# An LSTM with a low-rank adapter behind it: up product with tokens on partitions, and the residual added on TensorE

## The chip, the cores and the metric

The kernel runs on one core of one Trainium2 chip. The metric is the device time of an execution in microseconds (us). The median of three runs of the kernel before is 622.96 us (622.89 to 625.73).

## The reference

`x` has 16 batches of 256 tokens with 256 channels, all float32. First an LSTM runs over the 256 tokens, and its hidden states are added to `x`. Then an adapter, whose low-rank parts (rank 8) are made per batch from a condition vector, is applied, again with a residual.

```
def _L0_cond_ref(x, h0, Wx, Wh, b):
    xz = einsum('ntd,dk->ntk', x, Wx) + b
    step: z = xz_t + prev_h @ Wh;  ai, af, ao, ag = split(z, 4)
          i, f, o = sigmoid(ai), sigmoid(af), sigmoid(ao);  g = tanh(ag)
          next_c = f * prev_c + i * g;  next_h = o * tanh(next_c)

def _L1_cond_ref(x, ada_emb, base_up, base_down, ...):
    c = layernorm(ada_emb) * ln_gamma + ln_beta
    w = gelu(c @ W1 + bias1) @ W2 + bias2
    a1, b1, a2, b2 = [t.reshape(B, D, R) for t in split(w, 4)]
    u = einsum('btd,bdr->btr', x, a2)
    mid = gelu(einsum('btd,dl->btl', x, base_down) + einsum('btr,blr->btl', u, b2))
    v = einsum('blr,btl->btr', b1, mid)
    out = einsum('btl,kl->btk', mid, base_up) + einsum('bkr,btr->btk', a1, v)
    return x + out

x = x + _L0_cond_ref(x, cond_1024, Wx, Wh, b)
x = x + _L1_cond_ref(x, cond_1024, ...)
```

## The kernel before

The 256 tokens are cut into 32 blocks of `TB` = 8 tokens. A block of 8 tokens by 16 batches is 128 columns (or rows), which fills a 128-wide tile. `schedule` calls `one_block(k, front)` for every block on every engine; each engine has its own instruction stream, written out by hand, and the streams meet through semaphores. `front` is true for blocks 0 to 29. Inside a block there is a loop over the 8 recurrence steps `s`.

**The recurrence.** In each step PE computes the gates' inputs z from the hidden state h_t and `wh` (line 674: 32 narrow weight loads and products into the two `z` banks, then 16 into the `z_o` bank, each a 16-column tile). VectorE (DVE) transposes them (lines 821 and 825), ScalarE (ACT) takes the tanh of the gates (412, 418), VectorE makes products and the new cell (831, 836), ScalarE takes its tanh (424), and VectorE writes the two halves of h_t (843). PE waits for the first half before it starts the next z. Between z_o and the next z, PE's stream holds other work, called the filler here.

**The filler.** In front blocks one 256-wide piece of the input projection of block k + 2 closes every step's filler (`project`, line 496, bank `x_bank`). From block 4 on the adapter of the block before (`a = follower(k)`, lane 0) goes through the steps: `down_rank` in step 0 (u; line 507), `down_full` in steps 1 to 3 (six 128x128 products; line 522), `up_rank` in step 4 (v; line 529), `up_full` in steps 5 to 7 (six 128x128 products, channels on the partitions; line 545). All matmuls are float32. A float32 product appears in the trace as two LDWEIGHTS and two MATMUL instructions, a transpose as one of each. VectorE masks u and v (line 762), ScalarE does the GELU (346).

**The end of the adapter.** The up product leaves channels on partitions and tokens in the columns, in `out_bank`. `add_residual` (line 777, VectorE) adds `a.xp` (x + h of the block) and writes `y_t`. For blocks 4 to 28 that runs in step 2 of the block after, `transpose_y` (line 553, PE) turns its two halves in steps 3 and 4 back into `out_bank`, first in the filler, and `copy_y` (line 354, ScalarE) copies the result to `y_nat` in step 4, from where SP stores it. In the last blocks (`deferred` is false) the add is in step 6 of the same block, one transpose in step 7 and the other in step 0 of the block after.

**Early blocks.** The adapter's weights are not ready in the first blocks, so the adapter work of blocks 0 to 2 (`EARLY`) is kept for the end: `early(k)`, lane 1, with the bank `x_bank[1]` for the up product and `x_bank[0]` (free of projections then) for the rest, in blocks 30, 31 and in the tail behind the last block. There PE does `down_full(e)` as five products in step 1 and one in step 2. The tail is written out by hand: down, rank and up products of the last early block and of block 31, then adds, transposes and copies. `last_early` and `last` are these two jobs.

**POOL** adds h to x for each block (`add_h`, line 934) behind the last step of the block; before it overwrites `xp` it waits for the job that read it.

Of the kernel before, what the change touches and what calls it, by code (L numbers as in the profile page):

```python
# [54 lines left out]
def lstm_adapter(nc, x, cond, Wx, Wh, b, base_up, base_down, gamma, beta, W1, bias1, W2, bias2, out):  # L55
    ctx = ExitStack()
    with ctx:
# [64 lines left out]
        y_t = [sb(f"y_t{i}", [P, NM, P]) for i in lanes]  # L122
# [51 lines left out]
        out_psum, y_ready = ([sem(f"{n}{i}") for i in lanes] for n in ("out_psum", "y_ready"))  # L174
        yt_psum, y_copied = ([sem(f"{n}{i}") for i in lanes] for n in ("yt_psum", "y_copied"))
# [49 lines left out]

        def deferred(k):

            return k.plus(-1).k < NBLK - 2
# [91 lines left out]
        def _(act):  # L320
# [21 lines left out]
            def gelu_mid(a):  # L342
                act.wait_ge(mid_psum[a.lane], a.seq.k + 1)
                if a.seq.at_least(1):
                    act.wait_ge(out_psum[a.lane], a.seq.k)
# [4 lines left out]
            def copy_y(a):  # L350
                act.wait_ge(yt_psum[a.lane], a.seq.k + 1)
# [51 lines left out]
            def one_block(k, front):  # L403
                a, e, done = follower(k), early(k), follower(k.plus(-1))
                for s in range(TB):
# [47 lines left out]
                    if s == (4 if deferred(k) else 0) and done and done.seq.exists():  # L453
# [15 lines left out]
        def _(pe):  # L469
# [63 lines left out]
            def up_full(a, parts):  # L533

                for i in parts:
                    m, part = divmod(i, 3)
                    if i == 0:
# [4 lines left out]
                    cols = slice(m * P, (m + 1) * P)  # L542
                    lhs, rhs = ((up_t[:, part, cols], act_t[a.lane][:, part, :]) if part < 2 else
                                (a1_t[:, cols], v_own[a.lane][:, :]))
                    ins = pe.matmul(up_bank[a.lane][:, cols], lhs, rhs, start=(part == 0), stop=(part == 2))  # L545
                    if i == 5:
                        ins.then_inc(out_psum[a.lane], 1)

            def transpose_y(a, halves):
                if 0 in halves:  # L550
                    pe.wait_ge(y_ready[a.lane], a.seq.k + 1)
                for m in halves:
                    ins = pe.transpose(up_bank[a.lane][:, m * P:(m + 1) * P], y_t[a.lane][:, m, :], ident[:, :])  # L553
                if 1 in halves:
                    ins.then_inc(yt_psum[a.lane], 1)
# [87 lines left out]
            def one_block(k, front):  # L643
# [3 lines left out]
                for s in range(TB):  # L647
# [47 lines left out]
                    if a:  # L695
# [37 lines left out]
            transpose_y(follower(Blk(NBLK // 2 - 1, 1)), (1,))  # L733

# [237 lines left out]
```

## Time and profile before

| | |
|---|---|
| median of 3 runs | 622.96 us |
| the profiled execution | 622.3 us |
| its span, first to last instruction | 620.3 us |
| mean granted TensorE clock | 0.994 of full speed |
| PE busy | 600.6 us (97%) |
| PE weight loads (PEld) busy | 441.2 us (71%) |
| DVE busy | 478.7 us (77%) |
| ACT busy | 386.7 us (62%) |
| POOL busy | 38.2 us (6%) |

The times are of one execution on the chip. PE's products are pipelined and overlap, and their ends are modelled, so a busy PE is not one that has no room: how long an instruction occupies PE is read from the distance of starts. PEld is the weight load, which overlaps the products. An engine's idle time is given in brackets in the timeline, with what ended it. Where a helper records the operation its line is the helper's.

### The profile page before, as it was taken

What the parts mean: (1) busy time and instruction counts of PE and PEld (TensorE: products, weight loads), DVE (VectorE), ACT (ScalarE), POOL (GpSimd) and SP (SyncE); (2) the same over time, 40 slices, a digit from 0 to 9 for tenths busy, and PEclk for the clock granted to TensorE, in tenths of its full rate; (3) what the DMA queues carried; (4) which work ended last, traced back from release to release, by engine and by line L of the source; (5) the groups of instructions that cost most, each with busy time, mean ns of one, the idle gap of its engine ahead of it and who ended that gap; (6) DMA issues with size and microseconds to landing.
All of it is one profiled execution on the core that took longest, in us unless ns stands there. A gap on an engine that the chain in (4) does not pass through costs nothing.

```text
span 620.3 us, 34579 instructions
## 1 busy us (share of the span) xinstructions
PE 600.6 (97%) x14176; PEld 441.2 (71%) x14176; DVE 478.7 (77%) x2548; ACT 386.7 (62%) x2158; POOL 38.2 (6%) x78
## 2 busy tenths in 40 slices
PE   8789999999999999999999999999999999999997
PEld 5565555777777777777777777777777777777886
DVE  3566666888888888888888888888888888888773
ACT  2365555666666666666666666666666666666662
POOL 3000000000000000000000000000000000000000
PEclk9799999999999999999999999999999999999999
DMA  5893530232222113232321232322023232321201
GB/s 159 231 218 142 180 45 12 38 46 54 55 54 39 35 39 54 55 54 54 54 36 25 53 54 54 54 54 45 26 43 54 55 54 54 54 37 21 47 20 35
DMA packets 31471, 38.74 MB, mean 62 GB/s; under 512 B 3601, under 2 KB 29505, under 8 KB 30290
## 3 DMA queue, kind: packets, MB, share of 16 engines
q1 hardware_dynamic: 31282, 36.51, 27.4%
q8 instruction: 112, 1.84, 1.3%
q14 instruction: 45, 0.37, 0.2%
q0 software_dynamic: 32, 0.03, 0.0%
HBM read 15.55 MB, written 4.19 MB: 32 GB/s over the span
## 4 chain that ended last, share of the span: by engine, by line
PE 85%; DVE 7%; POOL 4%; issue 2%; DMA 1%; SPq 0%; POOLq 0%; ACT 0%; DVEq 0%; ACTq 0%
PE z L674 32%; PE x_bank L496 17%; PE aux L522 8%; PE z_o L674 7%; PE out_bank L545 5%; PE out_bank L603 4%; POOL xp L934 4%; PE aux L507 3%; PE aux L474 2%; PE out_bank L553 2%; PE aux L529 2%; DVE z L821 2%; DVE prod L831 1%; DVE gates L836 1%; DVE h_t L843 1%
## 5 line engine op out<-in xcount | busy, mean ns | idle before, releaser
L674 PEld LDWEIGHTS z<-wh,h_t 128*16 128x16 f32 x8160 | 155.1, 96 | 119.6 <-DVE h_t L843 96.0
L674 PE MATMUL z<-wh,h_t 128*16 128x96 f32 x8160 | 228.1, 248 | 5.6 <-DVE h_t L843 2.3
L821 DVE STREAM_TRANSPOSE z<-z 128x96 f32<-128x96 f32 x512 | 151.5, 298 | 87.2 <-PE z L674 60.3
L412 ACT ACTIVATE gates<-z 128x48 f32<-128x48 f32 x512 | 107.7, 210 | 141.9 <-DVE z L821 114.3
L496 PE MATMUL x_bank<-wx,x_t 128*128 128x256 f32 x512 | 156.2, 393 | 0.5 <-ACT x_t L330 0.5
L336 ACT ACTIVATE z<-seed 128x96 f32<-128x96 f32 x512 | 123.7, 242 | 5.6 <-DMA seed<-proj 5.6
L674 PE MATMUL z_o<-wh,h_t 128*16 128x64 f32 x4080 | 105.7, 219 | 0.4
L831 DVE SCALAR_TENSOR_TENSOR prod<-gates 128x32 f32<-128x32 f32 x512 | 97.8, 191 | 0.6
L836 DVE SCALAR_TENSOR_TENSOR gates<-prod 128x16 f32<-128x16 f32 x512 | 84.3, 165 | 8.7
L496 PEld LDWEIGHTS x_bank<-wx,x_t 128*128 128x128 f32 x512 | 80.7, 195 | 6.4 <-issue 1.5
L674 PEld LDWEIGHTS z_o<-wh,h_t 128*16 128x16 f32 x4080 | 80.6, 97 | 1.2 <-issue 0.9
L340 ACT ACTIVATE z_o<-seed 128x64 f32<-128x64 f32 x256 | 58.3, 228 | 33.8 <-DVE h_t L843 2.3
L418 ACT ACTIVATE gate_o<-z_o 128x32 f32<-128x32 f32 x256 | 50.4, 197 | 29.2 <-DVE z_o L825 7.5
L825 DVE STREAM_TRANSPOSE z_o<-z_o 128x64 f32<-128x64 f32 x256 | 65.8, 257 | 0.5 <-PE z_o L674 0.4
L934 POOL TENSOR_TENSOR xp<-x_t,h_t 128x128 f32<-128x128 f32 x58 | 29.4, 528 | 494.0 <-DVE h_t L843 494.0
L756 DVE TENSOR_TENSOR proj<-x_bank,b_all 128x256 f32<-128x256 f32 x128 | 53.8, 420 | 5.3 <-PE x_bank L496 5.1
L843 DVE SCALAR_TENSOR_TENSOR h_t<-gate_o,tanc 128x16 f32<-128x16 f32 x256 | 43.8, 171 | 13.3 <-ACT tanc L424 1.2
L843 DVE SCALAR_TENSOR_TENSOR h_t<-gate_o,z_o 128x16 f32<-128x16 f32 x256 | 43.8, 171 | 9.2
L424 ACT ACTIVATE tanc<-gates 128x16 f32<-128x16 f32 x256 | 46.7, 182 | 0.0
L424 ACT ACTIVATE z_o<-gates 128x16 f32<-128x16 f32 x256 | 46.1, 180 | 0.1
L522 PE MATMUL aux<-xp,down 128*128 128x128 f32 x232 | 43.1, 288 | 0.0
L545 PE MATMUL out_bank<-act_t,up_t 128*128 128x128 f32 x232 | 42.8, 289 | 0.0
(109 smaller groups left out, 445.9 us busy)
## 6 DMA issues: line engine op xcount, KB each, us to landing
seed<-proj SPq DMA_DIRECT2D x128, 128.0 KB, 4.0
w<-in_L_cond_W SPq DMA_DIRECT2D x4, 2048.0 KB, 9.9
x_nat<-in_x SPq DMA_DIRECT2D x32, 128.0 KB, 4.0
out<-y_nat SPq DMA_DIRECT2D x32, 128.0 KB, 3.7
wx<-in_L_cond_Wx SPq DMA_DIRECT2D x2, 512.0 KB, 5.6
wh<-in_L_cond_Wh SPq DMA_DIRECT2D x2, 256.0 KB, 6.5
wh<-in_L_cond_Wh SPq DMA_DIRECT2D x1, 512.0 KB, 6.2
w<-in_L_cond_W SPq DMA_DIRECT2D x1, 256.0 KB, 4.3
```

What stands on the lines that cost most here:

```text
L336: act.activation(z_bank[m][:, 0:GC], seed[buf][:, s, GC * m:GC * (m + 1)], ACT.Copy)\
L412: act.activation(gates[s % 2][m][:, 0:3 * B].rearrange("p (g b) -> p g b", b=B), zt[m].rearrange("p (g c) -> p g c", c=C)[:, :, 0:B], ACT. ...
L424: act.activation(tanc[m], gates[(s + 1) % 2][m][:, 3 * B:4 * B], ACT.Tanh, scale=0.5).then_inc(tanc_ready[m], 1)
L496: ins = pe.matmul(x_bank[q % 2][:, 0:XW], x_t[f.k % N_X][:, kc, :], wx[:, kc, q * XW:(q + 1) * XW], start=(kc == 0), stop=(kc == 1))
L522: ins = pe.matmul(mid_bank[a.lane][:, cols], lhs, rhs, start=(part == 0), stop=(part == 2))
L545: ins = pe.matmul(up_bank[a.lane][:, cols], lhs, rhs, start=(part == 0), stop=(part == 2))
L674: ins = pe.matmul(dst, h_prev[:, kc, :], rhs, start=False, stop=(kc == 1), skip_group_check=True)
L821: dve.transpose(zt[m], z_bank[m][:, 0:GC]).then_inc(turned[m], 1)
L825: dve.transpose(zt_o, o_bank[:, 0:OC]).then_inc(turned_o, 1)
L831: dve.scalar_tensor_tensor(prod[m][:, :], now[:, 0:2 * B], 1.0, now[:, 2 * B:4 * B], ALU.add, ALU.mult).then_inc(prod_ready[m], 1)
L836: dve.scalar_tensor_tensor(gates[(s + 1) % 2][m][:, 3 * B:4 * B], prod[m][:, B:2 * B], 0.5, prod[m][:, 0:B], ALU.mult, ALU.add).then_inc(c ...
L843: dve.scalar_tensor_tensor(h_t[k.par][:, m, s, 0:B], gate_o[:, B * m:B * (m + 1)], 1.0, tanc[m], ALU.add, ALU.mult).then_inc(ht_ready[m], 1)
```

## The change

The up product is turned around: the activations (and the masked v) are now the stationary operand and `up_t` (and `a1_t`) the moving one, 256 columns wide, so that tokens come out on the partitions. Three wide products take the place of six narrow ones. The residual is added in the same PSUM region, by two products with `a.xp` as the stationary operand and the identity as the moving one (`x0`, `x1`, 128 columns each). `add_residual`, `y_t` and `transpose_y` are gone. In front blocks l0, l1 and v are in steps 5, 6 and 7, x0 and x1 in steps 3 and 4 of the block after; block 30 follows the same plan, in block 31 x0 and x1 come in step 7. The GELU that overwrites `act_t` waits for l1 alone (`act_used`). The early blocks' down product is three and three, the first rank product of `last_early` moves from step 7 to step 6 of block 31 with its mask, and the tail is in another order.

```diff
-            def up_full(a, parts):
-                for i in parts:
-                    m, part = divmod(i, 3)
...
-            def transpose_y(a, halves):
...
+            def up_full(a, parts, whole=False):
+                y = up_bank[a.lane]
+                for part in parts:
+                    if part == "l0":
+                        if a.seq.at_least(1):
+                            pe.wait_ge(y_copied[a.lane], a.seq.k)
+                        pe.wait_ge(up_ready, 2)
+                        pe.wait_ge(act_ready[a.lane], a.seq.k + 1)
+                    if part == "v":
                         pe.wait_ge(v_ready[a.lane], a.seq.k + 1)
...
+                    lhs, rhs, lo = {"l0": (act_t[a.lane][:, 0, :], up_t[:, 0, :], 0),
+                                    "l1": (act_t[a.lane][:, 1, :], up_t[:, 1, :], 0),
+                                    "v": (v_own[a.lane][:, :], a1_t[:, :], 0),
+                                    "x0": (a.xp[:, 0, :], ident[:, :], 0),
+                                    "x1": (a.xp[:, 1, :], ident[:, :], P)}[part]
+                    width = P if part in ("x0", "x1") else D
+                    ins = pe.matmul(y[:, lo:lo + width], lhs, rhs, start=(part == "l0"),
+                                    stop=(whole and part == parts[-1]), skip_group_check=True)
+                    if part == "l1":
+                        ins.then_inc(act_used[a.lane], 1)
+                if whole:
+                    ins.then_inc(y_psum[a.lane], 1)
...
-                    if done and done.seq.exists():
-                        if not deferred(k) and s == 0:
-                            transpose_y(done, (1,))
-                        if deferred(k) and s in (3, 4):
-                            transpose_y(done, (s - 3,))
-                    if s == 7 and not front and k.p == 1:
+                    if done and done.seq.exists() and s in (3, 4):
+                        up_full(done, ("x0",) if s == 3 else ("x1",), whole=(s == 4))
+                    if s == 6 and not front and k.p == 1:
                         pe.wait_ge(v_ready[1], last_early.seq.k)
                         down_rank(last_early)
...
-                        if front and s in (5, 6, 7):
-                            up_full(a, range(2 * s - 10, 2 * s - 8))
-                        if not front and s in (5, 6):
-                            up_full(a, range(3 * s - 15, 3 * s - 12))
-                        if not front and s == 7:
-                            transpose_y(a, (0,))
+                        if s >= 5:
+                            up_full(a, (("l0",), ("l1",), ("v",))[s - 5])
+                        if s == 7 and not front and k.p == 1:
+                            up_full(a, ("x0", "x1"), whole=True)
...
                         if s in (1, 2):
-                            down_full(e, range(0, 5) if s == 1 else range(5, 6))
+                            down_full(e, range(3 * s - 3, 3 * s))
...
                         if s in (4, 5, 6):
-                            up_full(e, range(2 * s - 8, 2 * s - 6))
+                            up_full(e, (("l0",), ("l1",), ("v",))[s - 4])
                         if s == 7:
-                            transpose_y(e, both)
+                            up_full(e, ("x0", "x1"), whole=True)
...
             schedule(one_block)
-            transpose_y(follower(Blk(NBLK // 2 - 1, 1)), (1,))
-            down_full(last_early, range(0, 4))
+            down_full(last_early, range(6))
             down_rank(last)
-            down_full(last_early, range(4, 6))
-            down_full(last, range(0, 3))
             up_rank(last_early)
-            down_full(last, range(3, 6))
-            up_full(last_early, range(0, 3))
+            down_full(last, range(6))
+            up_full(last_early, ("l0", "x0", "x1"))
             up_rank(last)
-            up_full(last_early, range(3, 6))
-            up_full(last, range(6))
-            transpose_y(last_early, both)
-            transpose_y(last, both)
+            up_full(last_early, ("l1", "v"), whole=True)
+            up_full(last, ("l0", "x0", "x1", "l1", "v"), whole=True)
...
-            def add_residual(a):
-                dve.wait_ge(out_psum[a.lane], a.seq.k + 1)
-                dve.tensor_tensor(y_t[a.lane][:, :, :], a.xp[:, :, :],
...
                 if k.at_least(EARLY + 2):
-                    pool.wait_ge(y_ready[0], k.k - EARLY - 1)
+                    pool.wait_ge(y_psum[0], k.k - EARLY - 1)
```

## Rows read from the trace of the kernel before

**Rows 1.** The page's chain by engine; who waited for whom (us, times, longest).

```profile
PE 85%; DVE 7%; POOL 4%; issue 2%; DMA 1%; SPq 0%; POOLq 0%; ACT 0%; DVEq 0%; ACTq 0%
...
PEld z L674 <- DVE h_t L843: 96.0, 242, 0.9
```

**Rows 2.** Timeline, block 15, steps 3 to 6: start, us, engine, line, operation.

```profile
309.63 0.67 PEld L674 LDWEIGHTS z<-wh,h_t 128*16 128x16 f32 x32 [0.42 <-DVE h_t L843]
...
309.71 0.41 DVE L777 TENSOR_TENSOR y_t<-xp,out_bank 128x256 f32<-128x256 f32 x1
...
310.69 0.33 PE L553 MATMUL out_bank<-ident,y_t 128*128 128x128 f32 x1
...
310.86 0.39 PE L522 MATMUL aux<-xp,down 128*128 128x128 f32 x2
...
311.30 0.60 PE L496 MATMUL x_bank<-wx,x_t 128*128 128x256 f32 x2
...
311.62 0.17 DVE L843 SCALAR_TENSOR_TENSOR h_t<-gate_o,tanc 128x16 f32<-128x16 f32 x1
...
311.85 0.67 PEld L674 LDWEIGHTS z<-wh,h_t 128*16 128x16 f32 x32 [0.35 <-DVE h_t L843]
...
316.27 0.67 PEld L674 LDWEIGHTS z<-wh,h_t 128*16 128x16 f32 x32 [0.35 <-DVE h_t L843]
```

**Rows 3.** Timeline of PE: last projection product before z, steps 3 and 0.

```profile
311.52 0.38 PE L496 MATMUL x_bank<-wx,x_t 128*128 128x256 f32 x1
...
304.95 0.38 PE L496 MATMUL x_bank<-wx,x_t 128*128 128x256 f32 x1
305.25 0.28 PE L674 MATMUL z<-wh,h_t 128*16 128x96 f32 x4
```

**Rows 4.** Timeline, block 15, step 2: first two products of the filler.

```profile
308.47 0.49 PE L522 MATMUL aux<-u_own,b_t 128*128 128x128 f32 x2
...
308.80 0.39 PE L522 MATMUL aux<-xp,down 128*128 128x128 f32 x2
```

**Rows 5.** Lines 553 and 545: durations in ns, min/median/max.

```profile
L553 PE MATMUL x_bank<-ident,y_t x6: 272/273/273, 588.9 to 616.2; 128*128 128x128 f32 x6
...
L545 PE MATMUL out_bank<-v_own,a_t x116: 275/275/377, 121.2 to 615.9; 128*128 128x128 f32 x116
```

**Rows 6.** Timeline of PE's weight loads, block 31, steps 5 to 7.

```profile
601.68 0.67 PEld L674 LDWEIGHTS z<-wh,h_t 128*16 128x16 f32 x32 [0.19 <-DVE h_t L843]
...
604.05 0.62 PEld L674 LDWEIGHTS z<-wh,h_t 128*16 128x16 f32 x32
...
605.05 0.52 PEld L545 LDWEIGHTS out_bank<-act_t,up_t 128*128 128x128 f32 x4
...
606.36 0.13 PEld L674 LDWEIGHTS z<-wh,h_t 128*16 128x16 f32 x8
```

**Rows 7.** Timeline, starts of z in block 30: steps 1 to 3, and block 31.

```profile
573.49 0.66 PEld L674 LDWEIGHTS z<-wh,h_t 128*16 128x16 f32 x32
...
576.28 0.63 PEld L674 LDWEIGHTS z<-wh,h_t 128*16 128x16 f32 x32
...
578.45 0.67 PEld L674 LDWEIGHTS z<-wh,h_t 128*16 128x16 f32 x32 [0.42 <-DVE h_t L843]
...
589.99 0.67 PEld L674 LDWEIGHTS z<-wh,h_t 128*16 128x16 f32 x32 [0.91 <-DVE h_t L843]
```

**Rows 8.** Timeline, block 30, step 5: first half of h_t.

```profile
585.22 0.17 DVE L843 SCALAR_TENSOR_TENSOR h_t<-gate_o,tanc 128x16 f32<-128x16 f32 x1 [0.40 <-ACT tanc L424]
```

**Rows 9.** Timeline of the tail.

```profile
607.37 0.52 PEld L507 LDWEIGHTS x_bank<-xp_early,a_w 128*128 128x128 f32 x4
...
610.96 0.38 ACT L346 ACTIVATE act_t<-x_bank 128x256 f32<-128x256 f32 x1 [1.85 <-PE x_bank L522]
...
617.20 0.38 ACT L354 ACTIVATE y_nat<-out_bank 128x256 f32<-128x256 f32 x1 [0.35 <-PE out_bank L553]
```

**Rows 10.** The page's group of the projection's bias add: busy, mean ns.

```profile
L756 DVE TENSOR_TENSOR proj<-x_bank,b_all 128x256 f32<-128x256 f32 x128 | 53.8, 420 | 5.3 <-PE x_bank L496 5.1
```

More of the change, by code:

```diff
@@ L121, in lstm_adapter @@
         act_t = [sb(f"act_t{i}", [P, 2, P]) for i in lanes]
-        y_t = [sb(f"y_t{i}", [P, NM, P]) for i in lanes]
         y_nat = [[sb(f"y_nat{lane}_{i}", [P, D]) for i in range(2)] for lane in lanes]
@@ L173, in lstm_adapter @@
         v_psum, v_ready = ([sem(f"{n}{i}") for i in lanes] for n in ("v_psum", "v_ready"))
-        out_psum, y_ready = ([sem(f"{n}{i}") for i in lanes] for n in ("out_psum", "y_ready"))
-        yt_psum, y_copied = ([sem(f"{n}{i}") for i in lanes] for n in ("yt_psum", "y_copied"))
+        act_used = [sem(f"act_used{i}") for i in lanes]
+        y_psum, y_copied = ([sem(f"{n}{i}") for i in lanes] for n in ("y_psum", "y_copied"))
         stored = [[sem(f"stored{lane}_{i}") for i in range(2)] for lane in lanes]
@@ L224, in early @@
             return Job(Blk(0, 0, n), 1) if 0 <= n < EARLY else None
-        def deferred(k):
-            return k.plus(-1).k < NBLK - 2
         end = Blk(NBLK // 2, 0)
@@ L344, in gelu_mid @@
                 if a.seq.at_least(1):
-                    act.wait_ge(out_psum[a.lane], a.seq.k)
+                    act.wait_ge(act_used[a.lane], a.seq.k)
                 act.activation(act_t[a.lane][:, :, :],
@@ L350, in copy_y @@
             def copy_y(a):
-                act.wait_ge(yt_psum[a.lane], a.seq.k + 1)
+                act.wait_ge(y_psum[a.lane], a.seq.k + 1)
                 if a.seq.at_least(2):
@@ L452, in one_block @@
                         gelu_mid(a)
-                    if s == (4 if deferred(k) else 0) and done and done.seq.exists():
+                    if s == 4 and done and done.seq.exists():
                         copy_y(done)
@@ L531, in up_rank @@
                 ins.then_inc(v_psum[a.lane], 1)
-            def up_full(a, parts):
-                for i in parts:
-                    m, part = divmod(i, 3)
-                    if i == 0:
+            def up_full(a, parts, whole=False):
+                y = up_bank[a.lane]
+                for part in parts:
+                    if part == "l0":
                         if a.seq.at_least(1):
@@ L540, in up_full @@
                         pe.wait_ge(up_ready, 2)
+                        pe.wait_ge(act_ready[a.lane], a.seq.k + 1)
+                    if part == "v":
                         pe.wait_ge(v_ready[a.lane], a.seq.k + 1)
[L542 to L547, printed above, removed]
-            def transpose_y(a, halves):
[L550 to L555, printed above, removed]
+                    lhs, rhs, lo = {"l0": (act_t[a.lane][:, 0, :], up_t[:, 0, :], 0),
[10 more added lines that the diff above has]
+                    ins.then_inc(y_psum[a.lane], 1)
             def make_weights(k, s):
@@ L772, in mask_v @@
                 mask(mid_bank[a.lane], v_own[a.lane], v_ready[a.lane])
-            def add_residual(a):
-                dve.wait_ge(out_psum[a.lane], a.seq.k + 1)
-                dve.tensor_tensor(y_t[a.lane][:, :, :], a.xp[:, :, :],
-                                  up_bank[a.lane][:, 0:NM * P].rearrange("p (m t) -> p m t", m=NM), ALU.add)\
-                   .then_inc(y_ready[a.lane], 1)
             dve.memset(zeros[:, :], 0.0).then_inc(zeroed, 1)
@@ L864, in one_block @@
             def one_block(k, front):
-                a, e, f, done = follower(k), early(k), k.plus(2), follower(k.plus(-1))
+                a, e, f = follower(k), early(k), k.plus(2)
                 for s in range(TB):
@@ L877, in one_block @@
                     new_hidden(k, s, 0, n)
-                    if s == 7 and not front and k.p == 1:
+                    new_hidden(k, s, 1, n)
+                    if s == 6 and not front and k.p == 1:
                         mask_u(last_early)
-                    new_hidden(k, s, 1, n)
                     if s == 0 and a:
@@ L889, in one_block @@
                         mask_v(a)
-                    if s == 2 and deferred(k) and done and done.seq.exists():
-                        add_residual(done)
-                    if s == 6 and a and not front:
-                        add_residual(a)
-                    if s == 6 and e:
-                        add_residual(e)
                     if not k.at_least(1) and s < 2:
@@ L908, in _ @@
             mask_v(last)
-            add_residual(last_early)
-            add_residual(last)
         @block.gpsimd
```

## The prediction

> **What bounds the kernel now.** I read the chain of waits first, then who waits for whom. The chain is 85% PE, but in the second view PE waits for the hidden state 242 times [rows 1]: in most of the 256 recurrence steps PE's other work, the "filler" issued behind the gate products, is done before h_t. So I went to the timeline of one ordinary block. There a step lasts 2.21 to 2.22 us (z loads at 309.63 and 311.85; three steps on, at 316.27, 6.64 after the first). The half of h_t that PE waits for ends at 311.62 + 0.17 = 311.79 and z follows 0.06 later: the loop h_t, z, transpose, gates, cell, h_t sets the step. Filler starts 1.06 after z (310.69) [rows 2].
>
> How much room has the filler? The last x_bank product of that step starts at 311.52, 0.33 before z. In the step where POOL holds the filler up and PE is late, the same product starts 0.30 before z (304.95, 305.25) [rows 3]. So in the steps whose filler is a transpose, two narrow products and the projection, PE has only 0.03 us to spare. What an edit adds to PE in such a step lengthens it; what it takes off VectorE counts only where h_t or a transpose has waited for it.
>
> **The change, part by part.**
>
> 1. *Residual add on VectorE goes* (32 of 0.41 us). It begins at 309.71 behind h_t and ends at 310.12, and the next gate transpose can't begin before z's products are through; the step with it is as long as the others [rows 2]. Hidden by that wait, so worth 0. Bounds: 0 and a gain of 0.41 each, if it had held a transpose up, which the equal step lengths exclude in the ordinary blocks. The two of the tail are in part 5.
>
> 2. *Up product with tokens on partitions, steps 5 to 7.* Six 128-wide products (12 PE instructions) become three 256-wide ones (6). A narrow instruction costs 0.11 in a stream: the four of two narrow products take 0.44 (310.86 to 311.30). A wide one has the x_bank product as its row: its halves start at 311.30 and 311.52, 0.22 apart [rows 2, 3]. 12 x 0.11 = 1.32 against 6 x 0.22 = 1.32: PE time is the same, and the steps wait for h_t anyway. Worth 0; bounds -0.1 to +0.1 per block in PE time, and 0 in the step time while the 0.03 holds.
>
> 3. *Two transposes become two identity products, steps 3 and 4 of the next block.* They stand first in the filler. A transpose is one instruction, and the product behind it starts 0.17 later (310.69, 310.86) [rows 2]. An ordinary narrow product is two instructions, and when it stands first, the product behind it starts 0.33 later (308.47, 308.80) [rows 4]. So each swap costs 0.16 of PE where 0.03 is free. The move of the residual from VectorE, which had room, to PE, which has none, is the core of the case.
>
> Step by step, with ten narrow instructions of filler as the nearest rows (1.10 by 0.11 each; the new filler, six narrow and two wide, is 0.66 + 0.44, the same). Such filler runs 1.31 from its start to z (605.05, 606.36), of which 0.21 is getting started and the way out; I take 1.30 for the new one. Step 3: 1.06 + 1.30 = 2.36. Step 4 starts with z late, so that both halves of h_t are there and its filler starts 1.00 after z (604.05, 605.05) [rows 6]: 1.00 + 1.30 = 2.30. Step 5 gets 0.04 back, 2.17, as after the other late step (576.28, 578.45) [rows 7]. Sum 6.83 against 6.64: +0.19 per block. The pair of measured steps agrees: 2.37 and 2.31 with ten instructions [rows 6]. Blocks 5 to 29 do this, 25 of them: **+4.8 us**. Bounds: 0, if the swap costs no more than the 0.03, and 25 x 2 x 0.16 = +8.0, if no lateness comes back. I take 4.8, since the row of a late step shows what comes back.
>
> Two rules of the Trainium skill bear on this swap, and they pull apart. "TensorE: Matmul & The Clock Gate", Part 4, prices a 128x128 transpose at some 275 ns in a kernel, most of it latency; the trace's duration of a transpose, 0.273, agrees, and it is that of an ordinary narrow product, 0.275 [rows 5], so by this rule the swap costs nothing and the 25 blocks add 0. "FP8 and Floating Point Precision", TensorE Precision Notes, says true FP32 takes four passes through the array; an estimate from it is three more passes of 128 columns at 2.4 GHz, 0.16 per swap, which gives the 4.8. Starts, not durations, say how long PE is taken, and they side with the second.
>
> 4. *Blocks 30 and 31, where early blocks 0 and 1 are worked in beside the last ones.* Early down product: ten instructions in step 1 and two in step 2 become six and six. Block 30 from z at 573.49 to 589.99 is 16.50 now, with 2.79 in step 1 [rows 7]. New: step 1 has ten instructions, 1.04 + 1.31 = 2.35; step 2 ten and late, 2.32; step 3 ten (identity, down, rank), 2.32; step 4 six narrow and two wide, 2.31; step 5 four wide, 2.17, plus the 0.36 by which VectorE paused there in this execution [rows 8], 2.53; steps 6 and 7 2.21 and 2.23 as an ordinary and as the present one. Sum 16.27: **-0.23**. The pause is left in both, being no part of the change. Block 31 up to z at 606.36 is 16.37 now. New: 2.34 for step 0 as now, 2.32 three times, 2.31, 2.17, and 2.56 for step 6, which gains the first rank product of the last early block: four narrow and four wide, 0.63 + 0.41 + 1.51. Sum 16.34: **-0.03**. Bounds for both: -0.8 (every added ten-instruction step hidden) and +0.5 (a further late step in each).
>
> 5. *Tail.* From the start of the last step's filler to the last copy 617.20 - 607.37 = 9.83 pass [rows 9]. Afterwards PE runs 14 wide and 52 narrow instructions there, 14 x 0.22 + 52 x 0.11 = 8.80 (wide: v of block 30's job and both last up products; narrow: eight identity instructions there and eight later, the two down products with 24, three groups of four for rank products). It must stop for the first GELU, whose rank product now stands right behind four instructions: that GELU takes 0.38 (610.96) [rows 9], and with 0.4 of handing over on both sides (my estimate from the 0.06 that PE needs after h_t and the 0.28 that a product takes to come out) 0.78 pass, against 0.56 of PE's other work: 0.22. Starting up, semaphores and the last product's way out I put at 0.5. Sum 9.52. Gone are the residual add and the transposes at the very end, but the full early down product now stands ahead of the last block's rank product and eats most of that. **-0.3**, bounds -1.0 (no stop, add and transposes all gained) and +0.6 (a second stop as long as the first plus a semaphore).
>
> 6. *Waits.* The identity products need no wait (a.xp and the bank are ready), the l0 product waits for act_t alone, and the v mask is asked for two steps later: all come later than what they wait for. POOL's h add waits for y_psum of step 4 instead of y_ready of step 2; it is asked for after step 7, over 6 us later. On ACT the copy stands at the same place. Worth 0, bounds 0 and 0.1 per block.
>
> Sum: 4.8 - 0.23 - 0.03 - 0.3 = +4.2 us. The profiled span 620.3 becomes 624.5, its execution 622.3 becomes 626.5. The median shown is 0.66 above that execution, so I predict **627.2** (+0.7%).
>
> **The rivals.**
>
> *A, the swap is free.* PE loads the weights of the identity product, which waits for nothing, while the z_o products still run, or a transpose occupies PE as long as its duration says. Then step 3 stays at 2.21 and only parts 4 and 5 count: 622.96 - 0.56 = **622.4**, not slower. For it: equal durations [rows 5]. Against: the down product that stands first in rows 4 waits for nothing either and still has its 0.33. It decides once the swap costs under 0.07 (0.03 room, and 0.04 that come back).
>
> *B, the late step also blocks VectorE.* In step 3 VectorE adds the bias to the projection, 0.42 long [rows 10], once the last x_bank product is through. With PE late that is z - 0.30 + 0.38 = z + 0.08, so the add ends near z + 0.52, and the gate transpose wants VectorE at z + 0.59. If the signal comes more than 0.07 later than I count, the transpose waits too: say 0.1 per block, 25 x 0.1 = 2.5, **629.7**. Against: the 0.07 are there by the rows.
>
> *C, half is paid.* The lateness of step 3 is not carried into step 4, because pauses of other engines or the copies' places widen the room: 0.10 per block, **624.9**.
>
> **How the numbers follow.** Forecast 0.64, A 0.16, B 0.08, C 0.12. About 0.5% (3.1 us) is what a measurement of this kernel can tell from no change. Slower by more: nearly all of the forecast (its own range is 625.0 to 629.2) and B, 0.69. Within: A, C and a rest of the forecast, 0.27. Faster by more: 0.04, if the pauses of 0.36, of which there are a handful, fall away on top of A. The range 622.3 to 629.4 takes A in and leaves out B and the tails.
>
> **What would show it.** Right: in the middle blocks steps 3 and 4 last 2.35 and 2.30, with z 0.19 behind the end of h_t instead of 0.06, step 5 lasts 2.17 and the rest 2.21, and a block is 17.96 instead of 17.77. The identity product takes 0.33 before its neighbour. Wrong: steps 3 and 4 stay at 2.21 (A), or the idle time of VectorE before the gate transpose of step 4 is gone and the transpose starts over 0.63 after z (B). In blocks 30 and 31 step 1 must fall from 2.8 to 2.35.

## The result, and the profile after

The changed kernel takes 628.5 us (median of 4 executions, 627.69 to 629.49) against 623.2 us for the kernel before on the same chip: ratio 1.0072, 95% interval 1.0041 to 1.0104. It is slower by some 0.7%, with an interval clear of 1, and lies within the forecast's range (627.2 us, 622.3 to 629.4). The profiled execution took 627.69 us with a span of 625.9, at a mean granted clock of 0.995 (before: 0.994), so the clock has no part in the difference of the two profiles.

The page after, sections 1 and 4 (busy time of the engines; the chain by engine):

```profile
span 625.9 us, 34291 instructions
...
PE 606.4 (97%) x14048; PEld 445.3 (71%) x14048; DVE 469.9 (75%) x2516; ACT 387.1 (62%) x2158; POOL 38.3 (6%) x78
...
PE 86%; DVE 6%; POOL 4%; issue 2%; DMA 1%; SPq 0%; POOLq 0%; ACT 0%; DVEq 0%; ACTq 0%
```

And who waited for whom (us, times, longest):

```profile
PEld z L669 <- DVE h_t L820: 97.3, 246, 0.9
```

VectorE has 8.8 us less to do than before (469.9 against 478.7) and the kernel is 5 us slower. These rows don't say why. The waits for the hidden state still look as in [rows 1], 246 times instead of 242, though in 50 of these steps PE itself is now late. The list counts every weight load that had to wait at all, and in the late steps, too, it shows 0.33 us of idle time put down to h_t (below, 333.00). The lengths of the steps have to be read. The timeline of an ordinary block (16; start, us, engine, line, operation; z of steps 3, 4, 5 and 6 and what stands in step 3; answers to [rows 2]):

```profile
330.65 0.67 PEld L669 LDWEIGHTS z<-wh,h_t 128*16 128x16 f32 x32 [0.42 <-DVE h_t L820]
...
331.70 0.49 PE L545 MATMUL out_bank<-ident,xp 128*128 128x128 f32 x2
...
332.03 0.39 PE L517 MATMUL aux<-xp,down 128*128 128x128 f32 x2
...
332.47 0.60 PE L491 MATMUL x_bank<-wx,x_t 128*128 128x256 f32 x2
...
332.64 0.17 DVE L820 SCALAR_TENSOR_TENSOR h_t<-gate_o,tanc 128x16 f32<-128x16 f32 x1
...
333.00 0.63 PEld L669 LDWEIGHTS z<-wh,h_t 128*16 128x16 f32 x32 [0.33 <-DVE h_t L820]
...
333.11 0.42 DVE L740 TENSOR_TENSOR proj<-x_bank,b_all 128x256 f32<-128x256 f32 x1
...
333.59 0.63 DVE L798 STREAM_TRANSPOSE z<-z 128x96 f32<-128x96 f32 x2
...
335.31 0.63 PEld L669 LDWEIGHTS z<-wh,h_t 128*16 128x16 f32 x32 [0.33 <-DVE h_t L820]
...
337.48 0.67 PEld L669 LDWEIGHTS z<-wh,h_t 128*16 128x16 f32 x32 [0.37 <-DVE h_t L820]
```

Step 3 lasts 2.35 (330.65 to 333.00), step 4 2.31, step 5 2.17. The first half of h_t ends at 332.64 + 0.17 = 332.81 and z follows 0.19 later, where in [rows 2] it followed after 0.06: PE is what ends last. The identity product begins at 331.70 and the next product at 332.03, 0.33 later, where the transpose of [rows 2] let its neighbour start after 0.17. From the start of the filler to z pass 1.30 us.

The durations don't give this price. The group of the identity products (line 545, durations in ns, min/median/max), and that of the transposes before, in the same bank (line 553):

```profile
L545 PE MATMUL out_bank<-ident,xp x116: 273/275/377, 133.2 to 621.6; 128*128 128x128 f32 x116
...
L553 PE MATMUL out_bank<-ident,y_t x58: 273/329/333, 132.3 to 616.9; 128*128 128x128 f32 x58
```

58 identity products give 116 instructions with a median of 275 ns; the 58 transposes gave 58 with a median of 329. The 273 of [rows 5] is that of six transposes in the other bank. At the head of a filler a transpose takes 329 ns, and a product's first instruction 377; behind other products the two take 273 and 275. None of these is the time for which PE is taken: that is read from the starts.

Starts of z in blocks 30 and 31 (steps 1 to 6 of block 30, step 0 and step 7 of block 31), to be held against [rows 7] and [rows 6]:

```profile
580.13 0.62 PEld L669 LDWEIGHTS z<-wh,h_t 128*16 128x16 f32 x32
...
582.45 0.63 PEld L669 LDWEIGHTS z<-wh,h_t 128*16 128x16 f32 x32
...
584.77 0.62 PEld L669 LDWEIGHTS z<-wh,h_t 128*16 128x16 f32 x32
...
587.09 0.63 PEld L669 LDWEIGHTS z<-wh,h_t 128*16 128x16 f32 x32
...
589.39 0.63 PEld L669 LDWEIGHTS z<-wh,h_t 128*16 128x16 f32 x32 [0.33 <-DVE h_t L820]
...
591.56 0.67 PEld L669 LDWEIGHTS z<-wh,h_t 128*16 128x16 f32 x32 [0.43 <-DVE h_t L820]
...
596.05 0.67 PEld L669 LDWEIGHTS z<-wh,h_t 128*16 128x16 f32 x32 [0.27 <-DVE h_t L820]
...
612.37 0.62 PEld L669 LDWEIGHTS z<-wh,h_t 128*16 128x16 f32 x32 [0.33 <-DVE h_t L820]
```

The tail: its first filler product, the GELU of the last early block, the product that waits for it, the last copy (answers to [rows 9]):

```profile
613.38 0.30 PEld L545 LDWEIGHTS out_bank<-a_t,v_own 128*128 128x128 f32 x2
...
616.34 0.39 ACT L341 ACTIVATE act_t<-x_bank 128x256 f32<-128x256 f32 x1 [0.68 <-PE x_bank L517]
...
616.78 0.52 PEld L524 LDWEIGHTS x_bank<-act_t,b_w 128*128 128x128 f32 x4 [0.22 <-ACT act_t L341]
...
622.80 0.38 ACT L349 ACTIVATE y_nat<-out_bank 128x256 f32<-128x256 f32 x1 [1.36 <-PE out_bank L545]
```

The balance of the two profiled spans, from the starts of z (us). "Scattered" is what blocks 5 to 29 took beyond 25 times the sum of their median steps:

| stretch | before | after | difference | forecast |
|---|---|---|---|---|
| start to z of block 5 | 124.38 | 125.47 | +1.09 | 0 |
| blocks 5 to 29, 25 x (17.767; 17.961) | 444.17 | 449.03 | +4.85 | +4.8 |
| the same blocks, scattered | 2.69 | 3.29 | +0.60 | 0 |
| block 30 | 18.75 | 18.26 | -0.49 | -0.23 |
| block 31 to z of its step 7 | 16.38 | 16.32 | -0.06 | -0.03 |
| from there to the last copy | 10.83 | 10.43 | -0.40 | -0.3 |
| last copy to the end | 3.08 | 3.07 | -0.01 | 0 |
| span | 620.3 | 625.9 | +5.6 | +4.2 |

### The profile page after: what moved, and what is told of

The parts are those of the page before. It is cut to its first block, busy times and chain, and to the rows that moved or that the text cites. A ratio compares the mean times of both kernels' runs of the same rounds, so it can differ in the third digit from the quotient of the medians.

```text
span 625.9 us, 34291 instructions
## 1 busy us (share of the span) xinstructions
PE 606.4 (97%) x14048; PEld 445.3 (71%) x14048; DVE 469.9 (75%) x2516; ACT 387.1 (62%) x2158; POOL 38.3 (6%) x78
## 4 chain that ended last, share of the span: by engine, by line
PE 86%; DVE 6%; POOL 4%; issue 2%; DMA 1%; SPq 0%; POOLq 0%; ACT 0%; DVEq 0%; ACTq 0%
PE z L669 31%; PE x_bank L491 17%; PE out_bank L545 9%; PE aux L517 8%; PE z_o L669 7%; POOL xp L903 4%; PE out_bank L598 4%; PE aux L502 3%; PE aux L469 2%; PE aux L524 2%; DVE z L798 2%; DVE prod L808 1%; DVE gates L813 1%; DVE h_t L820 1%; DVE z_o L802 1%
## 5 line engine op out<-in xcount | busy, mean ns | idle before, releaser
L669 PEld LDWEIGHTS z<-wh,h_t 128*16 128x16 f32 x8160 | 156.9, 96 | 116.5 <-DVE h_t L820 97.3
L491 PEld LDWEIGHTS x_bank<-wx,x_t 128*128 128x128 f32 x512 | 87.2, 196 | 10.7 <-issue 1.5
L545 PE MATMUL out_bank<-up_t,act_t 128*128 128x256 f32 x116 | 35.1, 385 | 0.0
```

Source lines behind the costliest of these rows:

```text
L491: ins = pe.matmul(x_bank[q % 2][:, 0:XW], x_t[f.k % N_X][:, kc, :], wx[:, kc, q * XW:(q + 1) * XW], start=(kc == 0), stop=(kc == 1))
L545: ins = pe.matmul(y[:, lo:lo + width], lhs, rhs, start=(part == "l0"), stop=(whole and part == parts[-1]), skip_group_check=True)
L669: ins = pe.matmul(dst, h_prev[:, kc, :], rhs, start=False, stop=(kc == 1), skip_group_check=True)
```

## The experiments

My theory: the whole loss is the kind of PE work that the residual is made of. Where a step's filler has 0.03 us to spare, two instructions in place of one make it late, and the place in the block hardly matters. The turned up product and the add taken off VectorE are worth nothing. The rivals: the late steps come from the wide products or their neighbourhood; the add's going is a gain that something eats; the identity product's price is one of its place behind z_o. All step lengths below are medians over blocks 5 to 29, from the starts of z, as in the balance; the kernel before has 2.32 2.17 2.21 2.21 2.21 2.21 2.21 2.21 for steps 0 to 7. Each ratio is to the kernel before on the same chip; its medians in the three sets were 623.55 (e1 to e4), 623.71 (a0_again, e5 to e7) and 623.14 (e8, e1_again). A ratio isn't the quotient of the two medians (in a0_again that is 1.0059, the ratio 1.0048), but every interval holds both.

### e1_transpose_acc: the changed kernel with the residual as accumulating transposes

```diff
                     ins = pe.matmul(y[:, lo:lo + width], lhs, rhs, start=(part == "l0"),
+                                    is_transpose=(part in ("x0", "x1")),
```

> The changed kernel, with x0 and x1 as float32 transposes that accumulate onto the up product (one PE instruction each instead of two); nothing else differs, VectorE still adds nothing. My theory (the swap costs 0.16 us of PE where 0.03 is free): the filler of steps 3 and 4 runs 1.14 instead of 1.30, these steps fall from 2.35 and 2.31 to 2.21, a middle block from 17.96 to 17.77 (-4.9 us over 25 blocks), and with the fewer instructions in blocks 30, 31 and the tail the kernel comes to 622.4 us, ratio to before about 0.999. Rival (the loss comes from the wide products, the missing wait or the other order of the work, not from the identity products): it stays near 628.

Measured: 622.43 us, ratio 0.9978 [0.9958, 0.9998] (two of the twelve executions took 1063 and 2976 us; the ratio leaves them out, and without them the median is 622.09). Steps 3 and 4 are 2.213 and 2.212, the median block is 17.771. PE in step 3 of block 16:

```profile
329.67 0.33 PE L545 MATMUL out_bank<-ident,xp 128*128 128x128 f32 x1
...
329.84 0.39 PE L517 MATMUL aux<-xp,down 128*128 128x128 f32 x2
...
330.83 0.28 PE L670 MATMUL z<-wh,h_t 128*16 128x96 f32 x4
```

The count is x1, the neighbour starts 0.17 later, z 1.16 after the filler's start instead of 1.30. One word in one call takes the whole loss away; everything else of the change is still there.

### e2_before_product: the kernel before with its transposes as ordinary products

```diff
-                    ins = pe.transpose(up_bank[a.lane][:, m * P:(m + 1) * P], y_t[a.lane][:, m, :], ident[:, :])
+                    ins = pe.matmul(up_bank[a.lane][:, m * P:(m + 1) * P], y_t[a.lane][:, m, :], ident[:, :],
+                                    start=True, stop=True)
```

> The kernel before, with the two transposes of y done as ordinary products with the identity (two PE instructions each instead of one); the add on VectorE, the narrow up product and the old end stay. My theory: this alone makes steps 3 and 4 last 2.35 and 2.31, a middle block 17.96, +4.9 us, and some +0.4 in blocks 30 and 31: 628.5 us, ratio 1.0085. Rival (a transpose takes PE as long as a product, as their equal durations say): 623.2, no change.

Measured: 627.84 us, ratio 1.0064 [1.0044, 1.0083]; steps 3 and 4 2.349 and 2.306, block 17.961. Starts of z, steps 3 to 6 of block 16:

```profile
328.01 0.67 PEld L675 LDWEIGHTS z<-wh,h_t 128*16 128x16 f32 x32 [0.42 <-DVE h_t L844]
...
330.36 0.62 PEld L675 LDWEIGHTS z<-wh,h_t 128*16 128x16 f32 x32 [0.33 <-DVE h_t L844]
...
332.67 0.62 PEld L675 LDWEIGHTS z<-wh,h_t 128*16 128x16 f32 x32 [0.33 <-DVE h_t L844]
...
334.83 0.67 PEld L675 LDWEIGHTS z<-wh,h_t 128*16 128x16 f32 x32 [0.35 <-DVE h_t L844]
```

So the loss of the middle blocks can be put into the kernel before by this edit alone, to the hundredth of a step: 2.35, 2.31, 2.16. Together with e1 this is the cause from both sides.

### e3_before_balanced: the kernel before with the early down product three and three

```diff
-                            down_full(e, range(0, 5) if s == 1 else range(5, 6))
+                            down_full(e, range(3 * s - 3, 3 * s))
```

> The kernel before, with the early blocks' down product as three and three products in steps 1 and 2 instead of five and one. My theory: in blocks 30 and 31 step 1 falls from 2.80 and 2.77 to 2.36 and 2.32, step 2 rises from 2.17 to 2.32 and step 3 from 2.21 to 2.17 after a late step: -0.3 each, 622.6 us in all, too small for the clock but plain in the trace. Rival (the products of step 1 were hidden): no change of z's starts.

Measured: 622.21 us, ratio 0.9978 [0.9955, 1.0]. Starts of z in block 30, steps 1 to 4:

```profile
573.79 0.67 PEld L674 LDWEIGHTS z<-wh,h_t 128*16 128x16 f32 x32
...
576.15 0.62 PEld L674 LDWEIGHTS z<-wh,h_t 128*16 128x16 f32 x32
...
578.47 0.63 PEld L674 LDWEIGHTS z<-wh,h_t 128*16 128x16 f32 x32
...
580.64 0.67 PEld L674 LDWEIGHTS z<-wh,h_t 128*16 128x16 f32 x32
```

Steps 1 to 3 are 2.36, 2.32 and 2.17 where they were 2.80, 2.17 and 2.21: 0.33 less per block in blocks 30 and 31, 0.7 us in all. The trace shows the gain; the times can't show 0.7 us surely, as the interval ends at 1.0.

### e4_double: the identity products twice

```diff
-                        up_full(done, ("x0",) if s == 3 else ("x1",), whole=(s == 4))
+                        up_full(done, ("x0", "x0") if s == 3 else ("x1", "x1"), whole=(s == 4))
```

> The changed kernel, with x0 and x1 of the front blocks done twice in their steps (the residual counts twice there, so the result differs). My theory: steps 3 and 4 are PE-bound already, so each added narrow product costs its full 0.22: step 3 2.57, step 4 2.53, +0.45 per block and +11.2 us over the 25 blocks, +0.45 each in blocks 30 and 31 or a little less: about 640.5 us. Rival C of the prediction (room of some other kind swallows part of what is added): clearly less, 634 or so.

Measured: 638.41 us, ratio 1.0234 [1.0204, 1.0265]. Steps 3 and 4 are 2.570 and 2.530, block 18.405. Step 3 of block 16:

```profile
335.73 0.90 PE L669 MATMUL z<-wh,h_t 128*16 128x96 f32 x32
...
336.78 0.71 PE L545 MATMUL out_bank<-ident,xp 128*128 128x128 f32 x4
...
337.33 0.39 PE L517 MATMUL aux<-xp,down 128*128 128x128 f32 x2
...
338.30 0.34 PE L669 MATMUL z<-wh,h_t 128*16 128x96 f32 x5
```

The second product costs 0.22 a step, full price (0.55 to the neighbour's start instead of 0.33): once the room is gone each further narrow float32 product is paid whole, and the next step gives back no more than the 0.04. The 25 blocks account for 0.444 x 25 = 11.1 us over the changed kernel. Blocks 30 and 31 add 0.9 more (18.70 and 16.79 against 18.26 and 16.32), and the scattered time is 1.4 less (1.9 against 3.3). The total is 11.0 above the 627.4 that the next run gives for the changed kernel; the expected 640.5 had been built on its first median of 628.5 and was 2.1 too high.

### a0_again: the changed kernel a second time

> The changed kernel once more, beside the other three. Step theory: steps 3 and 4 of a middle block again 2.35 and 2.31, the kernel 627 to 629 us. Open is the stretch up to block 5, which took 1.1 us longer in the first profile than before: if that belongs to the change, it is there again; if it is the loading of the inputs, which varies from run to run, it lies anywhere between 123.4 and 125.5.

Measured: 627.37 us (10 executions), ratio 1.0048 [1.0024, 1.0072]. The steps are the same within 0.004 us (2.350, 2.306), but block 5 starts at 123.41, where it started at 125.47 in the first profile and at 124.38 in the kernel before. So the start-up of one kernel varies by 2 us, and the +1.09 of the balance's first line needs no effect of the change. It isn't excluded either: block 5 starts between 123.41 and 126.34 in the eight profiles without the add on VectorE, and between 123.42 and 124.50 in the four with it. The two sets put the loss at +0.5 and +0.7%, 3.7 and 5.3 us.

### e5_narrow: the wide up products cut in two

```diff
+                    halves = ((lo, lo + P),) if width == P else ((0, P), (P, D))
+                    for c, (at, to) in enumerate(halves):
+                        ins = pe.matmul(y[:, at:to], lhs, rhs if width == P else rhs[:, at:to],
```

> The changed kernel with each 256-wide product of the up product cut into two of 128 columns: twelve PE instructions in steps 5 to 7 again, tokens still on partitions. My theory (a wide instruction takes PE twice as long as a narrow one): the filler of steps 5 and 6 is 1.14 instead of 1.13, both under the 1.16 there are, steps stay 2.17 and 2.21, time 628.5, the same within 0.3 us. Rival (the wide products save or cost PE time): steps 5 to 7 change by over 0.02.

Measured: 626.93 us beside 627.37 for the uncut kernel on the same chip (1.006 [1.0039, 1.0081] and 1.0048 [1.0024, 1.0072]); the median block is 17.960 against 17.956. Twelve narrow instructions or six wide ones: no difference in these blocks, where steps 5 to 7 wait for h_t anyway. The cut does cost PE a little: in step 5 the last projection product starts 0.33 before z instead of 0.35, so the filler is nearly 0.02 longer, and in the tail, where PE ends last, the stretch from z of step 7 to the last copy is 10.53 in its profile against 10.43 in both of the uncut kernel.

### e6_added_step1: the same extra work in a step that had none

To e1 a transpose of 65536 times the identity and a product with its negative are added at the head of step 1's filler; together they add zero to the up bank, but for rounding on the diagonal. (The edit also makes the two tiles, once, at the start.)

```diff
+                    if front and done and done.seq.exists() and s == 1:
+                        pe.wait_ge(big_made, 2)
+                        pe.matmul(up_bank[0][:, 0:P], big[:, :], ident[:, :], start=False, stop=False,
+                                  is_transpose=True, skip_group_check=True)
+                        pe.matmul(up_bank[0][:, 0:P], minus_big[:, :], ident[:, :], start=False, stop=False,
+                                  skip_group_check=True)
```

> The kernel with x0 and x1 as accumulating transposes, and two more products added in step 1 of the front blocks, onto the same half of the bank: a transpose of 65536 times the identity and an ordinary product with minus it, which cancel. My theory: the filler of step 1 grows from 1.08 by 0.11 + 0.22 to 1.41; step 1, which starts late, goes from 2.17 to 2.42, step 2 gets 0.04 back, +0.20 per block, 25 blocks +5.1: 627.5 us. Rival (step 1 has room enough, as it has neither a transpose nor the residual): no change, 622.4.

Measured: 624.59 us, ratio 1.0016 [0.9984, 1.0049]. PE in step 1 of block 16:

```profile
326.84 0.33 PE L682 MATMUL out_bank<-ident,big 128*128 128x128 f32 x1
...
327.01 0.39 PE L684 MATMUL out_bank<-ident,minus_big 128*128 128x128 f32 x2
...
327.23 0.61 PE L522 MATMUL aux<-xp,down 128*128 128x128 f32 x4
...
328.20 0.34 PE L675 MATMUL z<-wh,h_t 128*16 128x96 f32 x5
```

Step 1 became 2.370, not 2.42, and step 2 2.169, so a block grows by 0.14 (3.6 us over the 25) instead of 0.20. The mechanism held, its size didn't. Filler to z is 1.36 here. The same filler without the pair (two narrow products and the projection) would take 1.07 if it set z: in step 1 of the kernel before, its last projection product starts 0.77 after its first product, and z follows 0.31 after that one where PE is late (here 2.370 - 2.063). So the pair costs 0.29. The product is 0.22 of it (327.01 to 327.23), which leaves 0.06 to 0.07 for the transpose, where I had set 0.11. A transpose at the head of the filler costs less than its distance to the neighbour, since that distance holds a delay that any first product has (0.33 - 0.22 = 0.11 for an ordinary one). The loss is read from the steps; the time's own interval holds 1, and the scattered time is 2 us less than in e1's profile (3.0 against 5.0).

### e7_steps_1_2: the identity products in other steps

```diff
-                    if done and done.seq.exists() and s in (3, 4):
-                        up_full(done, ("x0",) if s == 3 else ("x1",), whole=(s == 4))
+                    if done and done.seq.exists() and s in (1, 2):
+                        up_full(done, ("x0",) if s == 1 else ("x1",), whole=(s == 2))
```

> The changed kernel with x0 and x1 in steps 1 and 2 of the block after instead of 3 and 4, where the filler without them is as long (1.08) and has the same 0.09 of room. My theory, that only the sum of the filler in a step counts: step 1 2.31, step 2 2.31, step 3 2.17, step 4 2.21, +0.19 per block as in steps 3 and 4: 628.3 us. Rival (the place matters: products that stand behind a late step are caught up): under 626.

Measured: 626.83 us, ratio 1.0043 [1.0017, 1.0069]. Starts of z in block 16, steps 1 to 4:

```profile
327.42 0.63 PEld L669 LDWEIGHTS z<-wh,h_t 128*16 128x16 f32 x32 [0.33 <-DVE h_t L820]
...
329.74 0.62 PEld L669 LDWEIGHTS z<-wh,h_t 128*16 128x16 f32 x32 [0.33 <-DVE h_t L820]
...
332.04 0.62 PEld L669 LDWEIGHTS z<-wh,h_t 128*16 128x16 f32 x32 [0.33 <-DVE h_t L820]
...
334.21 0.67 PEld L669 LDWEIGHTS z<-wh,h_t 128*16 128x16 f32 x32 [0.42 <-DVE h_t L820]
```

2.32, 2.30 and 2.17 here, as medians 2.306, 2.306 and 2.170, block 17.953: the lateness moves with the product, and a different place saves nothing. In blocks 30 and 31, whose steps 1 and 2 also hold the early down product, it costs: these steps become 2.54 instead of 2.32, 0.5 us for both blocks. Steps 1 to 3 all hold two narrow products and the projection, 1.07 of the 1.16 us between the filler's start and z. The 0.09 left take a transpose at the head (0.06 to 0.07, and 0.02 to 0.03 are over, the room of the forecast) and not a product (0.22, late by 0.13).

### e8_add_kept: the add back on VectorE, in a kernel with free transposes

To e1 the 128x256 add (of `xp` and the up bank) is put back in step 2, into a scratch tile, and PE waits for it before x0.

```diff
+                    if done and done.seq.exists() and s == 3:
+                        pe.wait_ge(peeked, done.seq.k + 1)
...
+                    if s == 2 and done and done.seq.exists():
+                        dve.wait_ge(v_in_y, done.seq.k + 1)
+                        dve.tensor_tensor(scratch[:, :, :], done.xp[:, :, :],
```

> The kernel with accumulating transposes, with the 128x256 add of the kernel before kept on VectorE in step 2 of the block after (into a scratch tile that nobody uses), and PE waiting for it before x0, as it did before. My theory (the add lies in time in which VectorE waits for z): step 2 and 3 stay 2.21, a middle block 17.77, the time is that of the kernel without it, 622.4 to 623. Rival (taking the add off VectorE gave something back, and the loss was larger than it looks): +0.1 to +0.4 per block, 625 or more. Beside it: the pauses of 0.36 between the gate transposes and h_t sat at block 12 step 0 and block 28 step 0 in all seven profiles of kernels without the add and at block 24 step 7 and block 30 step 5 in the two others and the one before; if they hang on the place in VectorE's instruction stream, they move back towards these here.

Measured: 620.57 us, ratio 0.9973 [0.9953, 0.9994], median block 17.764. The add is there, behind step 2's work on VectorE in block 16: z of step 3 starts at 326.14 and z of step 4 at 328.35, 2.21 later:

```profile
326.20 0.41 DVE L872 TENSOR_TENSOR scratch<-xp,out_bank 128x256 f32<-128x256 f32 x1
```

27 of the adds are back and no step is longer for them: with them the kernel is, if anything, quicker.

### e1_again: e1 on the chip of e8

> The kernel with accumulating transposes once more, for its ratio to before. By the steps it should differ from before only in blocks 30 and 31 and the tail, about -1.5 us by the first profiles: ratio 0.9975, and pauses again at block 12 step 0 and block 28 step 0. If the first ratio of 0.9978 was chance, it comes out at 1.

Measured: 623.11 us, ratio 0.9992 [0.9972, 1.0012]. My expectation of 0.9975 lies in the interval, but the interval now holds 1 as well, so e1 is not shown to be faster than the kernel before. What the traces show is this: from z of block 30 to the last copy e1 takes 43.9 us against 46.0 before, so the end gains 2.0 us, and the scattered time of blocks 5 to 29 is 5.0 and 4.6 in its two profiles against 2.7. In e8 it is 3.1. About 1 us of the difference to before is in the pauses of VectorE that are told of at the end. Most of the rest is in PE's own stream, which stands between two gate products in a few steps, as here in step 3 of block 12 in e1_transpose_acc; e1_again has the same 0.45 of idle time before the same two products:

```profile
257.21 0.40 PE L670 MATMUL z_o<-wh,h_t 128*16 128x64 f32 x14
258.06 0.28 PE L670 MATMUL z_o<-wh,h_t 128*16 128x64 f32 x2 [0.45 <-issue]
```

That step is 0.69 longer than the others of its kind, in both. What PE does there isn't shown.

## Why the prediction was right

The forecast's mechanism held, step by step, and its sizes nearly so; the case was decided in part 3. That the second set's median, 627.37, lies 0.2 from the forecast is in part luck: the end came out 0.4 better than forecast, and the kernel before measured 0.8 more there than the 622.96 that the forecast started from.

**Part 1, the add.** Worth 0, as said: e8 puts it back in the middle blocks and nothing gets longer there (17.764 against 17.771 per block). Profile and run agree that the wait for z's products hides it.

**Part 2, the wide product.** Worth 0 in a block: e5 undoes the width with 17.960 against 17.956, and e2, which has the whole old up product beside the new kind of residual work, takes 17.961 as the changed kernel does.

**Part 3, the swap.** Forecast 2.36, 2.30 and 2.17 for steps 3 to 5 and +0.19 per block; measured medians 2.346, 2.306 and 2.172, +0.194. The terms of the swap come out as 0.22 for the product and 0.06 for the transpose, 0.16 as forecast, though the forecast took this difference from 0.33 and 0.17. e2 has the loss without the rest of the change, e1 has the rest without it. The room is nearer 0.02 than 0.03: the last projection product starts 0.328 before z in the step with the transpose and 0.307 in the late ones (medians). Of the two rules weighed there, the price by passes of "FP8 and Floating Point Precision" (the Trainium skill, TensorE Precision Notes) is the one that the runs bear out: its estimate was 0.16 per swap. The 275 ns of "TensorE: Matmul & The Clock Gate" (the Trainium skill, Part 4) agrees with the 273 of transposes behind other products. The forecast read its agreement from six of these alone; the 58 in `out_bank` have a median of 329. Neither is a price of PE time.

**Part 4, blocks 30 and 31.** The forecast steps of block 30 were 2.35, 2.32, 2.32, 2.31, then 2.17 without the pause; the rows above give 2.32, 2.32, 2.32, 2.30, 2.17 from step 1. Block 31 from 596.05 to 612.37 is 16.32, forecast 16.34. Steps 1 to 7 of block 30 took 15.92 (580.13 to 596.05) against 16.50 before. I forecast 16.27, with the pause of 0.36 in step 5 [rows 8] left in; without it that is 15.91, and in the profile after it isn't there. Step 0, which I had left alone, grew by 0.09 (2.25 to 2.34), so that the whole block gave -0.49.

**Part 5, the tail.** 622.80 - 613.38 = 9.42 where I had 9.52 (before 9.83). PE stops for the GELU as forecast: its next product comes at 616.78, 616.34 + 0.39 = 616.73 after it, and the bracket shows 0.22 of idle time, my figure for the stop. What made the rest 0.1 shorter isn't separated.

**Part 6, the waits.** The one wait of POOL that is put down to the up bank is that of the last add, at 614.66, and the second half of h_t, which it needs as well, ends at 614.69; PE's only stop behind it is the one for the GELU. Worth 0. The others of POOL's adds for `xp` wait for h_t, as before.

**The rivals.** A (the swap is free) falls by the rows of block 16 and by e2. Its step lengths are those of e1. That e1 also measured the 622.4 that I gave it, 622.43, is chance: its repeat gave 623.11, and it has fewer instructions in blocks 30, 31 and the tail than A supposes. Whether it would decide under 0.07, as I put it, isn't tested: no run has a price between 0 and 0.16. B (VectorE blocked as well) falls: with the bias add at 333.11 to 333.53 the gate transpose starts at 333.59, 0.59 after z, no later than the 0.63 of steps without lateness. Only 0.06 lie between the two, so it was near. C (half paid) falls with medians of 2.35 and 2.31.

What is left of the first profile, 5.6 against 4.2, is 1.1 before block 5, which a0_again shows to vary by more, 0.6 of scattered pauses, and the better end.

## What to carry to other kernels

Before moving work to an engine, measure how much room it has in the step that receives it, against a step in which it is known to be late: here 0.02 to 0.03 us a step decided 4 to 5 us, while 0.4 us on the other engine was worth nothing. Read what an instruction costs from the distance of starts, with its place in the stream (first or in the middle), since durations don't show it: 273 and 275 ns stood here for a transpose that cost 0.06 us and for one of the two instructions of a product that cost 0.22. Where a transposed operand has to be added to a float32 sum, try the transpose itself as the accumulating instruction before an identity product, and look at the result's values.

## What the runs showed of the hardware

**A float32 transpose as the accumulating instruction.** In e1 the transposes are issued with start off onto a bank with an open float32 sum, at one instruction each: 0.17 to the neighbour's start, with step 3 at 2.21, against 0.33 and 2.35 for the identity product. That they add to the sum and don't overwrite it is taken from the kernel's result; no trace can show it.

**Pauses at fixed places of the program.** In a few steps VectorE stands for some 0.4 us between the last product and h_t (0.34 more than elsewhere), with the wait put down to ACT's tanh, though that tanh has ended. In the changed kernel, step 0 of block 12 (VectorE and the tanh, timeline):

```profile
253.17 0.18 ACT L419 ACTIVATE tanc<-gates 128x16 f32<-128x16 f32 x1
...
253.22 0.17 DVE L813 SCALAR_TENSOR_TENSOR gates<-prod 128x16 f32<-128x16 f32 x1
...
253.80 0.17 DVE L820 SCALAR_TENSOR_TENSOR h_t<-gate_o,tanc 128x16 f32<-128x16 f32 x1 [0.41 <-ACT tanc L419]
```

The tanh ends at 253.35 and h_t starts 0.45 later. The same place in e8, which has the add:

```profile
250.07 0.18 ACT L421 ACTIVATE tanc<-gates 128x16 f32<-128x16 f32 x1
...
250.36 0.17 DVE L827 SCALAR_TENSOR_TENSOR h_t<-gate_o,tanc 128x16 f32<-128x16 f32 x1
```

There it starts 0.11 after the tanh. The kernels without the add (the changed one twice, e1 twice, e4, e5, e6, e7) pause in step 0 of blocks 12 and 28; those with it (before, e2, e3, e8) pause in step 7 of block 24 and step 5 of block 30, e8 after the add was put back into e1. One place is common to all twelve profiles, step 2 of block 3 (0.42 idle before h_t at 93.25 in the kernel before, 0.40 at 94.32 in the changed one), and up to there VectorE's stream is the same in all of them. ScalarE's instructions are the same in e1 and e8, VectorE's are not, and PE's differ by one wait, so the places most likely go with VectorE's stream. What VectorE does in these pauses isn't shown. The pause of [rows 8] is one of them, and it went away with a change that leaves VectorE's work in that step as it was. Two other kinds appear in the kernels without the add only: the gate transpose of step 0 of block 15 starts 1.06 after z instead of 0.71, and in step 6 of blocks 7 and 23 the second half of h_t starts 0.18 late, and the gate transpose with it (0.81 instead of 0.63 after z). Whether these places are the reason why e1 measured 0.9978 and 0.9992 and e8 0.9973 stays open: the intervals overlap, and of the 3.7 us between the profiled spans of e1_again and e8, 2.5 lie before block 5 and 1.5 in the scattered time.
